# A gather split over three issuing engines is given back to GpSimd alone

## The reference, cut to what matters

```python
h   = maximum(layernorm(x), 0)                    # x: (12500, 256) float32
agg = segment_sum(h[src], dst, num_segments=N)    # 200,000 edges: a gather of 1 KB rows
z   = (1 + eps_gin) * h + agg
t   = relu(batchnorm(z @ W1 + b1))                # W1: 256 x 512
out = x + relu(batchnorm(t @ W2 + b2 + h))        # W2: 512 x 256
```

## Time and profile before

| what | us |
|---|---|
| median of 3 runs | 2125.38 |
| lowest and highest of them | 2125.23, 2125.50 |
| the profiled execution's own time | 2120.47 |
| its span, from the first to the last instruction | 2118.7 |

### The profile page before, as it was taken

How to read it: one execution, slowest core, us unless ns; L and a number is a source line. 1 busy time by engine, 2 the same in 40 slices (tenths; PEclk the granted TensorE clock), 3 DMA queues, 4 the chain that set the end, 5 groups by cost and what they waited for, 6 DMA issues and landing times.

```text
span 2118.7 us, 28752 instructions
## 1 busy us (share of the span) xinstructions
PE 1416.2 (67%) x4835; PEld 905.3 (43%) x4835; DVE 768.2 (36%) x1947; ACT 338.6 (16%) x661; POOL 1432.0 (68%) x1522
## 2 busy tenths in 40 slices
PE   3556567656755656656666675576666576689998
PEld 2344345434433434434444443344444344464447
DVE  7677753223222322312222232222232232233447
ACT  6767751000000000000000000000000000014446
POOL 7777777777777777777777777777777777750000
PEclk7778888888878878978878787887788787899999
DMA  6667654444444444444444444544444444448438
GB/s 201 216 215 239 219 176 130 129 121 140 130 121 139 139 112 140 139 112 139 140 115 135 140 130 119 140 140 111 140 139 111 140 137 133 128 143 311 178 137 322
DMA packets 130683, 325.54 MB, mean 154 GB/s; under 512 B 34581, under 2 KB 60018, under 8 KB 127302
## 3 DMA queue, kind: packets, MB, share of 16 engines
q0 software_dynamic: 72576, 198.28, 32.8%
q1 hardware_dynamic: 45250, 98.79, 13.6%
q10 hardware_dynamic: 12676, 26.68, 4.1%
HBM read 271.56 MB, written 52.05 MB: 153 GB/s over the span
## 4 chain that ended last, share of the span: by engine, by line
POOL 64%; issue 21%; PE 11%; DMA 2%; ACT 1%; DVE 0%; SPq 0%; POOLq 0%; DVEq 0%
POOL arena L658 64%; PE ps L1450 7%; DMA arena<-h_rows,arena 2%; PE ps L1332 2%; PE ps L1464 1%; DMA arena<-t_T 1%; PE ps L1368 0%; PE ps L1406 0%; DMA arena<-in_src 0%; ACT arena L1280 0%; DVE arena L1065 0%; ACT aggT L1080 0%; SPq L440 0%; ACT arena L1086 0%; ACT arena L1084 0%
## 5 line engine op out<-in xcount | busy, mean ns | idle before, releaser
L658 POOL DMA_INDIRECT arena<-h_rows,arena x1275 | 1205.5, 945 | 389.0 <-issue 386.9
L1332 PE MATMUL ps<-arena 128*96 128x256 f32 x3024 | 953.9, 484 | 664.3 <-DMA arena<-h_rows,arena 510.5
L1332 PEld LDWEIGHTS ps<-arena 128*96 128x96 f32 x3024 | 628.0, 214 | 971.4 <-issue 713.7
L848 DVE TENSOR_TENSOR aggT<-aggT,ps 128x192 f32 x196 | 69.3, 354 | 1048.1 <-PE ps L1342 1039.8
L1159 ACT COPY arena<-ps 96x256 f32<-96x256 f32 x37 | 13.3, 359 | 1550.5 <-PE ps L1342 1513.5
L658 POOL DMA_INDIRECT arena<-in_x,arena x221 | 208.9, 945 | 67.3 <-issue 67.3
L1368 PE MATMUL ps<-arena 128*128 128x512 f32 (+3 forms) x412 | 186.3, 577 | 1.6 <-DVE arena L881 1.5
L1450 PE MATMUL ps<-arena,W2s 128*128 128x512 f32 (+1 forms) x400 | 168.1, 582 | 1.1 <-ACT arena L1280 1.1
L935 DVE TENSOR_TENSOR arena<-arena,ps 128x768 f32<-128x768 f32 x159 | 149.8, 942 | 0.0
L1111 ACT ACTIVATE arena<-arena,nb,mv 128x256 f32<-128x256 f32 x237 | 119.7, 587 | 81.8 <-DVE nb L752 81.8
L1450 PEld LDWEIGHTS ps<-arena,W2s 128*128 128x128 f32 x400 | 75.7, 190 | 93.5 <-issue 86.5
(11 more groups left out here) (99 smaller groups left out, 592.9 us busy)
## 6 DMA issues: line engine op xcount, KB each, us to landing
rl_odd<-h_rows SPq DMA_DIRECT2D x3072, 1.0 KB
W2s<-h_rows ACTq DMA_DIRECT2D x3072, 1.0 KB
arena<-t_T SPq DMA_DIRECT2D x24, 1024.0 KB, 4.8
t_T<-arena SPq DMA_DIRECT2D x46, 512.0 KB
arena<-h_rows,arena POOLq DMA_INDIRECT x1275, 2.8
arena<-in_x SPq DMA_DIRECT2D x27, 512.0 KB, 5.7
h_rows<-arena ACTq DMA_DIRECT2D x24, 512.0 KB, 3.8
out<-arena SPq DMA_DIRECT2D x23, 512.0 KB
```

Of the source, the lines that this page charges most:

```text
L658: nc.gpsimd.indirect_dma_start(out=rows[slot(g)][:, k, :], out_offset=None, in_=(x if g < H_FROM else h_dram)[:, :], in_offset=bass.Indire ...
L848: V.tensor_tensor(z, z, winT_ps, ALU.add).then_inc(s_add, 1)
L1332: last = T.matmul(win_ps[g % 2], sel[:, g % 2, k, :], rows_of(g, k), start=k == 0, stop=k == n - 1)
```

## The change

GpSimd gathers all 1563 tiles. SyncE and ScalarE fetch no rows, the table of byte offsets is neither made nor stored, and the waits for it are gone. W2 is loaded at the outset, right behind W1, and TensorE waits for both before its first group. The storing of t in halves is not touched.

```diff
-        at_dram = nc.dram_tensor("row_at", (EB, P, P), i32, kind="Internal").ap()
...
         def rows_of(g, k):
-            if sp_tile(g, k):
-                return sp_rows[sp_groups.index(g) % ROW_BUFS]
-            if act_tile(g, k):
-                return act_rows[act_groups.index(g) % ROW_BUFS]
             return rows[slot(g)][:, k, :]
...
             sp.dma_start(W1s[:, :, :], W1.rearrange("(k p) n -> p k n", p=P)).then_inc(s_w, 16)
+            sp.dma_start(W2s[:, :, :], W2.rearrange("(k p) n -> p k n", p=P)).then_inc(s_w, 16)
...
-            sp.wait_ge(s_at, 1)
-            sp.dma_start(at_dram.rearrange("b p e -> p b e"), tab_i[0]).then_inc(s_atd, 16)
...
-                    sp.wait_ge(s_atd, 16)
-                    load_at(0)
-                for j, m in pieces_of_pass(c):
-                    load_rows(j, m)
-
-            sp.wait_ge(s_agg, act_groups[-1] + 1)
-            sp.dma_start(W2s[:, :, :], W2.rearrange("(k p) n -> p k n", p=P)).then_inc(s_w, 16)
...
                     wait_apart(pool, s_trc[0], NTR)
-                    wait_apart(pool, s_atd, 16)
...
                 for k in range(tiles_of(g)):
-                    if sp_tile(g, k) or act_tile(g, k):
-                        continue
                     t = g * GT + k
...
             S.copy(tab_f[0], tab_i[0]).then_inc(s_tabf[0], 1)
-            act.wait_ge(s_tabf[0], 1)
-            S.activation(tab_i[0], tab_f[0], ACT.Copy, scale=float(ROW_BYTES)).then_inc(s_at, 1)
...
-                if g == H_ACT:
-                    wait_h(act)
-                if g >= H_ACT:
-                    for j, m in row_pieces(eighths(ACT_EIGHTHS, g - H_ACT), eighths(ACT_EIGHTHS, g - H_ACT + 1),
-                                           len(act_groups)):
-                        load_rows(j, m)
...
-            pe.wait_ge(s_w, 16)
+            pe.wait_ge(s_w, 32)
             for g in range(1, NG - 4):
                 step(g)
...
             keep_warm(12, 1)
-            pe.wait_ge(s_w, 32)
```

More of the change, by code:

```diff
@@ L39 @@
 X_EARLY = 16
-SP_EIGHTHS = 20
-ACT_EIGHTHS = 10
 H_FROM = 30
@@ L49 @@
 HALF_T = FB // 2
-ROW_BUFS = 3
-PIECE = 16
-AT_ONCE = 32
 QUAD = 4
-ROW_BYTES = 4 * D
 def ceil(a, b):
@@ L92, in sem @@
             return ctx.enter_context(nc.semaphore(name))
-        at_dram = nc.dram_tensor("row_at", (EB, P, P), i32, kind="Internal").ap()
-        x_bytes = x.rearrange("n d -> (n d)").bitcast(mybir.dt.uint8)
         h_dram = nc.dram_tensor("h_rows", (N, D), f32, kind="Internal").ap()
[L98 to L123, removed]
         t_dram = nc.dram_tensor("t_T", (NQ, P, FB, QN), f32, kind="Internal").ap()
@@ L208, in build @@
         W1s = piece[1].rearrange("p (k n) -> p k n", n=F)
-        assert COPIES_FROM % 2 == 1 and COPIES_FROM > max(H_ACT, 2 * H_NODES + 2, NQ + 2)
+        assert COPIES_FROM % 2 == 1 and COPIES_FROM > max(H_FROM - 1, 2 * H_NODES + 2, NQ + 2)
         W2s = sb("W2s", [P, FB, D])
@@ L217, in build @@
         rl_odd = rl[1].rearrange("p f n -> p (f n)")
[L218 to L222, removed]
         mv1 = sb("mv1", [P, FB, 2])
@@ L262, in build @@
         s_half = [[sem(f"s_half{g}_{h}") for h in (0, 1)] for g in range(LAST)]
[L263 to L267, removed]
         s_pl = [sem(f"s_pl{b}") for b in range(HB)]
@@ L300, in wait_apart @@
             eng.sem_inc(s_apart, 1)
[L302 to L308, removed]
         def half_rows(g, k):
             return s_half[g - NG + LAST][k // HALF_G]
-        def pool_tiles(g):
-            return sum(not sp_tile(g, k) and not act_tile(g, k) for k in range(tiles_of(g)))
         def slot(g):
@@ L322, in rows_of @@
         def rows_of(g, k):
-            if sp_tile(g, k):
-                return sp_rows[sp_groups.index(g) % ROW_BUFS]
-            if act_tile(g, k):
-                return act_rows[act_groups.index(g) % ROW_BUFS]
             return rows[slot(g)][:, k, :]
-        def row_pieces(first, end, tiles):
-            return [divmod(n, P // PIECE) for n in range(first, min(end, tiles * P // PIECE))]
         def batch_rows(b):
@@ L365, in wait_rows @@
         def wait_rows(eng, g):
[L367 to L373, removed]
+            eng.wait_ge(s_rows[g % RG], 16 * sum(tiles_of(j) for j in range(g % RG, g + 1, RG)))
         def tiles_of(g):
@@ L1182, in _ @@
                 act.wait_ge(s_gend, 1)
[L1184 to L1200, removed]
-                for k in range(PIECE):
-                    e = m * PIECE + k
-                    reg = row_regs.pop(0)
-                    at = act.snap(reg, donate=True, min_val=0, max_val=(N - 1) * ROW_BYTES)
-                    act.dma_start(act_rows[j % ROW_BUFS][e:e + 1, :].bitcast(mybir.dt.uint8),
-                                  h_bytes[bass.ds(at, ROW_BYTES)].rearrange("(p e) -> p e", p=1)
-                                  ).then_inc(s_actrows[j % ROW_BUFS], 16)
-                    act.free_register(reg)
-            act.wait_ge(s_atd, 16)
-            load_at(0)
             def step(g):
```

## The result

| | before | after |
|---|---|---|
| median of 4 runs, us | 2125.44 (2125.23 to 2125.89) | 2188.99 (2187.82 to 2190.04) |
| profiled execution: time, span | 2120.47, 2118.7 | 2187.82, 2185.8 |

The ratio is 1.0298, 95% interval 1.0284 to 1.0313: 63.6 us slower, where 63.8 were forecast.

What follows compares the result with a forecast made beforehand. The prediction took GpSimd's issuing of gathers as the bound: 51 added gathers cost 63.8 us, all other terms 0, so 2125.4 + 63.8 = 2189.2 us, 3.0% slower, range 2186 to 2193.

Steps and rivals of the forecast that it cites:

- GpSimd sets the pace, and each gather costs a step: Gather stage: GpSimd never idles, so 51 added gathers at 1.250 to 1.2506 us each add 63.8 us.
- The offset between profiled and timed executions: Whole kernel: runs' median lies 4.9 us above the profiled execution; assumed fixed, giving 2189.2 us.
- Row fetches give nothing back: Removing SyncE's and ScalarE's row fetches leaves GpSimd's step unchanged: 0 us, at most 0.8 us back.
- The quiet stretch: 1780.26 to 1879.05 us in the trace before, without row fetches: 79 gather steps of 1.2505 us, as in the whole stage.
- The rival that the DMA engines set the pace: Gather stage: same rows move, so GpSimd's step falls to 1.210 us and time stays 2125.4 us; chance 0.01.
- W2 and the table: Start and end: dropping the offset table and loading W2 behind W1, landing at 23.3 us, cost 0 us.
- The slack in the first groups: First groups: GpSimd's fifth group starts 2.13 us after TensorE's first product is ready, the next thing late without W2's cover.
- The forecast that no gap but the first passes 0.3 us: Sign in the profile after: GpSimd's gathers show no gap over 0.3 us except the first.
- at its worst, at the lower clock: TensorE's group takes about 8.2 us (5.91 + 0.33 + 1.91) against GpSimd's 10.0, so TensorE doesn't become the bound.
- The tail: From last gather to the end: stays 224.7 us, change 0, within 2 us either way.
- every rival it named: Four: GpSimd waits in first groups (0.02), DMA engines set pace (0.01), faster than before (0.01), tail shifts (0.05).

Runs made afterwards that it cites:

- chip 4: Chip of three follow-up runs: changed kernel again 2183.75 us against 2121.01 for the kernel before (1.0296), and two kernels with extra instructions (2183.48) or extra transfers (2184.34).
- chip 2: Chip with the kernel before at 3016.32 us: 64-row gathers 2489.77, W2 after the flag 2489.65, rows also fetched 3078.83, before without ScalarE's fetches 2937.58.
- extra transfers: Kernel before with GpSimd gathering all tiles; SyncE and ScalarE load 51 tiles' bytes for nobody, 16 rows per DMA: 2184.34 us, ratio 1.0298.
- chip 1: Chip with the kernel before at 2984.76 us: changed kernel 2475.55, before without ScalarE's fetches 2905.15, without SyncE's 2785.54, all gathered and rows also fetched 3035.13.
- chips 1 to 3: The follow-up chips where the kernel before took 2984.76, 3016.32 and 3014.93 us; the changed kernel itself was timed on the first: 2475.55 us, ratio 0.8303.

## Why the prediction was right, point by point

**GpSimd sets the pace, and each gather costs a step.** Shown. On chip 4, whose gathers take the 946 ns of the earlier trace rows, the last of the 1563 starts at 1957.7 us; 1957.8 was forecast. That it fits to 0.1 us is partly luck: the gathers of h begin at 305.2 us, 0.6 later than 300.8 + 3 x 1.25, and their step of 1.2500 in place of 1.2506 us gives 0.8 back. The difference of the medians there is 2183.75 - 2121.01 = 62.7 us, 1.1 less than forecast. The ratio is 1.0296 there and 1.0298 in the result, in executions with different steps.

**The offset between profiled and timed executions.** The forecast took 4.9 us as something that timing adds to a profile. The runs point to another thing: the profile of before came from an execution of 2120.47 us, and on chip 4 the kernel before, timed, took 2121.01. The profile after, from the result's own runs, has gathers of 949 ns. 2.5 ns over 1563 gathers are 3.9 us, which is what its last gather is later than forecast. So GpSimd's step differs by 0.2% between executions, and with it the time. It is not simply one step to a chip: on chip 2 the same gathers of x took 946 ns in the run with gathers of 64 rows and 949 in the one with the late W2. What sets it stays open. The 3.2 ns that 4.9 us over 1512 gathers make fit the same reading for the runs of before, but no trace of theirs was seen. The forecast's sum was hardly touched: 51 gathers at 1.2537 cost 63.9 in place of 63.8 us.

So the near hit of the median, 2188.99 against 2189.2 us, holds some luck. The profiled execution came out 3.5 us above its forecast, and the median only 1.2 us above the profiled execution where 4.9 were assumed; the two errors cancel. The four runs alone lie 2.2 us apart. What the result supports is the difference of 63.6 us, not the last tenths of the time.

**Row fetches give nothing back.** Shown as above, within 0.8 us in all. The quiet stretch had already said it. The rival that the DMA engines set the pace falls with it: it needed a step of 1.210 us, and on chip 4 the step was 1.2500. Between 1000 and 1100 us the DMA share fell from the 0.45 of the earlier trace rows to 0.40, with the same 81 gathers in the stretch:

```profile
1000.00:1100.00 100.00, 75.61 (x81) 0.79 0.40 120
```

**W2 and the table.** W2 landed well before TensorE needed it. SyncE issued it at 10.67 us and it took 8.8 us, so 19.5 against the 23.3 laid end to end in the forecast. TensorE's first group began at 37.13 instead of 36.73 us; W2 is not the reason, for with W2 loaded at the end (extra transfers) it began at 37.12:

```profile
W2s<-in_L_gnn_W SPq DMA_DIRECT2D x1, 512.0 KB, 8.8
```

```profile
10.67 0.75 SPq L383 DMA_DIRECT2D W2s<-in_L_gnn_W  x1
```

```profile
37.13 5.94 PE L1179 MATMUL ps<-arena 128*96 128x256 f32 x16 [3.85 <-issue]
```

**The slack in the first groups was misread, without harm.** The forecast gave 2.13 us before GpSimd's fifth group as the nearest limit. The sixth group has less: in the trace of before the second group's product was ready at 53.10 us and the sixth group started at 54.52, 1.4 us later. On chip 4 it was used up:

```profile
48.25 6.68 PE L1179 MATMUL ps<-arena 128*96 128x256 f32 x16 [5.73 <-ACT arena L992]
55.20 0.94 POOL L541 DMA_INDIRECT arena<-in_x,arena  x1 [1.33 <-PE ps L1179]
```

TensorE's granted clock stayed at 0.50 until 54.0 us there, the group took 6.68 us in place of 5.21 before, and GpSimd waited 1.33 us in place of 0.30. The forecast that no gap but the first passes 0.3 us failed there, at a price of 1.0 us.

The same row corrects another reading. The forecast took the 5.91 us of the earlier trace rows for a group "at its worst, at the lower clock" and came to 8.2 us against GpSimd's 10.0. But the granted clock in that trace was 0.50 only up to about 402 us and 0.85 from 402 to 404. A group nearly all at 0.50 takes 6.68 us, and the four products with W1 took 3.67 us instead of 1.91 on chip 1 (from 1014.05 us). A group wholly at the lower clock would thus take over 10 us, an estimate from these rows. TensorE didn't become the bound (in the result GpSimd's waits on it are three of 0.3 us), but the margin of 1.8 us that was to show this wasn't there.

**The tail.** 224.2 us in the result and 2181.9 - 1957.7 = 224.2 on chip 4, against 224.7.

**What the forecast did not have at all** is a chip on which GpSimd isn't the bound. On chips 1 to 3 the same change makes the kernel 17% faster. That lies outside every rival it named.

## What to carry to other kernels

Where the chain runs through one engine and its constant issue gap, multiply the count of added instructions by the step from start to start, not by the busy time, and check the step in a stretch where the thing that you remove is already absent. Before trusting an offset between profiled and timed executions, compare the duration of the most frequent instruction in both: a few ns on 1500 of them make several us. A split that moves work into thousands of small instructions on other queues was worth 3% on one chip and cost 20% (2984.76 against 2475.55 us) on another, so time it on more than one. And when a step of the argument needs an engine's time at the lower clock, read the granted clock of just that stretch first.

## What the runs showed of the hardware that was not expected

- On three of four chips there were stretches in which TensorE, VectorE and SyncE began one instruction in 0.7 or 1.4 us or none at all; VectorE and TensorE stood still together for 13 us. GpSimd's gathers kept their step of 1.25 us in the same stretch until they had to wait. The kernel before took some 860 us longer on chip 1 than on chip 4 (2984.76 - 2121.01 = 864) and the changed kernel some 290 (2475.55 - 2183.75 = 292). The loss was larger the more row fetches on SyncE and ScalarE a kernel had, and so the more instructions; which of the two counts was not separated. The cause isn't known.
- An indirect gather's price on GpSimd hardly depends on the number of rows: 946 ns for 128 rows of 1 KB, 899 for 64, and the same 0.30 us gap. The step was the same at DMA shares of 0.45 and 0.70.
- GpSimd's step differs between executions, 1.2500 against 1.2531 us for the same program, and on chip 2 the instruction took 946 ns in one kernel and 949 in another.
